# Edge lists loaded and keyed in two halves of columns, from two DMA queues, in a graph and mixture-of-experts kernel

## What is computed

```
def gnn(X, w_est, rows, cols):
    W = zeros((256, 256)).at[rows, cols].set(w_est)
    return X @ W

def ffn(x, gamma, beta, Wr, br, W1, b1, W2, b2):
    xn = layernorm(x) * gamma + beta
    logits = xn @ Wr + br                       # 8 experts
    top_vals, top_idx = top_k(logits, 2)
    w_full = softmax(top_vals) spread over the 8 experts
    y = 0
    for e in range(8):
        h = gelu(xn @ W1[e] + b1[e])            # 256 -> 512
        y = y + (h @ W2[e] + b2[e]) * w_full[:, e]
    return y

x = x + gnn(layernorm(x), edge_weight, src, dst)
x = x + ffn(layernorm(x), gamma, beta, Wr, br, W1, b1, W2, b2)
```

## Time and profile before

| | us |
|---|---|
| timed runs | 1067.57, 1066.40, 1067.41 (median 1067.41) |
| profiled execution, its own time | 1067.55 |
| its span, first to last instruction | 1065.8 |
| busy: TensorE / VectorE / ScalarE / GpSimd | 902.6 / 753.5 / 633.5 / 630.5 |
| mean granted TensorE clock, share of full speed | 0.919 |

### The profile page before, as it was taken

The page is one execution under the profiler, slowest core; times in us unless marked ns, Lnnn a source line. Parts: engine busy times, 40 slices in busy tenths (PEclk is TensorE's granted clock), DMA queues, the critical chain, the costliest instruction groups (busy, mean ns, idle before and its releaser), DMA issues. The chain is left out here.

```text
span 1065.8 us, 25585 instructions
## 1 busy us (share of the span) xinstructions
PE 902.6 (85%) x6756; PEld 842.6 (79%) x6757; DVE 753.5 (71%) x2311; ACT 633.5 (59%) x1324; POOL 630.5 (59%) x490
## 2 busy tenths in 40 slices
PE   1494698898986109999999999999999999999991
PEld 1123577777765109999999999999999999999991
DVE  4995798999984606777777777777777777777761
ACT  2244567666654006667667667667677677677661
POOL 3645057777777752465655655655756565656653
PEclk9797798989986559999999999999999999999996
DMA  4144457757654443465554554554654554555542
GB/s 123 56 127 150 135 161 228 225 195 243 210 168 158 148 162 72 73 99 87 82 95 73 93 94 80 82 96 73 93 92 79 83 95 79 92 85 81 93 67 30
DMA packets 95923, 121.47 MB, mean 114 GB/s; under 512 B 15198, under 2 KB 73734, under 8 KB 95752
## 3 DMA queue, kind: packets, MB, share of 16 engines
q0 software_dynamic: 39904, 53.56, 29.1%
q1 hardware_dynamic: 55976, 67.43, 21.9%
HBM read 51.94 MB, written 69.00 MB: 113 GB/s over the span
## 5 line engine op out<-in xcount | busy, mean ns | idle before, releaser
L574 POOL DMA_INDIRECT out_dram<-ysb,yid x210 | 382.6, 1822 | 283.6 <-ACT ysb L1342 132.9
L744 PE MATMUL psum<-xh,w1s 128*128 128x256 f32 x1680 | 310.9, 285 | 0.0
L744 PEld LDWEIGHTS psum<-xh,w1s 128*128 128x128 f32 x1680 | 257.1, 189 | 0.0
L558 POOL DMA_INDIRECT slots<-arena_z,pos x196 | 191.8, 978 | 89.8 <-issue 58.8
L757 PE MATMUL psum<-w2h,hl 128*128 x840 | 237.5, 283 | 0.0
L757 PE MATMUL psum<-w2l,hh 128*128 x840 | 237.3, 283 | 0.0
L757 PE MATMUL psum<-w2h,hh 128*128 x840 | 237.2, 282 | 0.0
L744 PE MATMUL psum<-xl,w1s 128*128 128x256 f32 x840 | 235.3, 280 | 0.0
L1159 DVE TENSOR_TENSOR hl<-hact,hh 128x512 fp32r<-128x512 f32 x210 | 145.6, 693 | 88.0 <-ACT hh L1206 87.8
L1206 ACT ACTIVATE xh<-psum 128x512 fp32r<-128x512 f32 x105 | 62.7, 597 | 221.3 <-PE psum L731 221.3
L1325 ACT ACTIVATE hact<-psum,b1T 128x256 f32<-128x256 f32 x420 | 174.5, 466 | 14.2 <-PE psum L744 2.8
(11 more groups left out here) (186 smaller groups left out, 1123.8 us busy)
## 6 DMA issues: line engine op xcount, KB each, us to landing
zin<-slots SPq DMA_DIRECT2D x105, 260.0 KB
arena_x<-in_x_dram SPq DMA_DIRECT2D x14, 512.0 KB, 5.4
out_dram<-arena_s SPq DMA_DIRECT2D x14, 512.0 KB
arena_z<-in_L_ffn_W_dram SPq DMA_DIRECT2D x24, 256.0 KB, 2.8
arena_x<-in_x_dram SPq DMA_DIRECT2D x13, 384.0 KB
out_dram<-arena_s SPq DMA_DIRECT2D x13, 384.0 KB
out_dram<-ysb,yid POOLq DMA_INDIRECT x210, 4.3
slots<-arena_z,pos POOLq DMA_INDIRECT x196
```

Of the source, the lines that this page charges most:

```text
L558: pool.indirect_dma_start(slots[:, :], bass.IndirectOffsetOnAxis(ap=pos[b][0:n, k, s:s + 1], axis=0), zg[b][0:n, s, :], None).then_inc(sen ...
L574: pool.indirect_dma_start(out[:, :], bass.IndirectOffsetOnAxis(ap=yid[u % MB][:, n:n + 1], axis=0), ysb[u % YB][:, n, :], None, compute_op ...
L744: last = nc.tensor.matmul(bank[2 + 2 * b + q][:, m * PAIR:(m + 1) * PAIR], w1s[b][:, w, k, hb * P:(hb + 1) * P], xs[b][:, k * PAIR:(k + 1) ...
```

## The change

The loads of src go out on SyncE's queue, those of dst on ScalarE's. Each list is loaded in two halves of columns (0 to 895 and 896 to 1699, seven blocks of 128 each, the last one short), each half still in two DMAs by rows. Each half has its own semaphore `raw_in[h]`, and VectorE makes the keys of the first half before it waits for the second. `keys_ready` is raised once for each half, and TensorE waits for it at block 0 and at block 7. The router constants stand ahead of the waits for `block_out` and `scratch_ready` instead of behind them. ScalarE runs a copy of one column into `first_gelu` before the first copy from PSUM, and the table load comes with that. What is computed stays the same.

```
--- before.py
+++ after.py
@@ -23,6 +23,7 @@
 EBLK = -(-ECOLS // P)
 ELAST = ECOLS - (EBLK - 1) * P
 EPARTS = ((0, 112), (112, EROWS))
+EHALF = ((0, 7 * P), (7 * P, ECOLS))
 HALF = 2
 EARLY = 1
 ROW0 = 9
@@ -267,7 +268,7 @@
         s_const = sem("s_const")
         dve_passed = sem("dve_passed")
         pool_passed = sem("pool_passed")
-        raw_in = sem("raw_in")
+        raw_in = [sem(f"raw_in{h}") for h in range(2)]
         small_in = sem("small_in")
         keys_ready = sem("keys_ready")
         score_zeroed = sem("score_zeroed")
@@ -350,15 +351,18 @@
         x_tiled = x[0:(TILES - 1) * P, :].rearrange("(n p) d -> p n d", p=P)
         out_tiled = out[0:(TILES - 1) * P, :].rearrange("(n p) d -> p n d", p=P)
 
+        def load_edges(engine, a, i):
+            rows = a.rearrange("(p c) -> p c", p=EROWS)
+            for h, (left, right) in enumerate(EHALF):
+                for lo, hi in EPARTS:
+                    engine.dma_start(raw[i].bitcast(a.dtype)[lo:hi, left:right], rows[lo:hi, left:right]).then_inc(raw_in[h], 16)
+
         block = ctx.enter_context(nc.Block())
 
 
         @block.sync
         def _(sp):
-            for i, a in enumerate((src, dst)):
-                rows = a.rearrange("(p c) -> p c", p=EROWS)
-                for lo, hi in EPARTS:
-                    sp.dma_start(raw[i].bitcast(a.dtype)[lo:hi, :], rows[lo:hi, :]).then_inc(raw_in, 16)
+            load_edges(sp, src, 0)
             sp.dma_start(wr[:, :, :], Wr.rearrange("(k p) e -> p k e", p=P)).then_inc(small_in, 16)
             with nc.allow_non_contiguous_dma(reason="two values a partition"):
                 sp.dma_start(gam[:, :], gamma.rearrange("(k p) -> p k", p=P)).then_inc(small_in, 16)
@@ -597,8 +601,9 @@
 
 
             pe.wait_ge(s_const, 4)
-            pe.wait_ge(keys_ready, 1)
             for i in range(EBLK):
+                if i % 7 == 0:
+                    pe.wait_ge(keys_ready, i // 7 + 1)
                 m = P if i < EBLK - 1 else ELAST
                 nc.tensor.transpose(bank[i // 4][0:m, (i % 4) * P:(i % 4) * P + EROWS],
                                     key_raw[:, i * P:i * P + m], ident[0:EROWS, 0:EROWS]).then_inc(block_turned, 1)
@@ -784,27 +789,27 @@
         @block.vector
         def _(dve):
             v = nc.vector
-            dve.wait_ge(raw_in, 32 * len(EPARTS))
             t = Steps(dve, edge_step, 0)
-
-
-            outer = junk[0:EROWS, 0:ECOLS]
             src_i, dst_i = raw[0].bitcast(I32), raw[1].bitcast(I32)
-            t.did(v.tensor_tensor(outer, src_i, dst_i, ALU.max))
-            t.then(v.scalar_tensor_tensor(out=src_i, in0=src_i, scalar=8, in1=dst_i, op0=ALU.logical_shift_left, op1=ALU.bitwise_or))
-            dve.wait_ge(s_const, 1)
-            t.then(v.tensor_tensor(src_i, src_i, place_raw, ALU.bitwise_or))
-            v.scalar_tensor_tensor(out=key_raw, in0=outer, scalar=float(D), in1=key_raw, op0=ALU.is_lt, op1=ALU.mult).then_inc(keys_ready, 1)
-            dve.wait_ge(block_out, 4)
+            for h, (left, right) in enumerate(EHALF):
+                def half(a):
+                    return a[0:EROWS, left:right]
+                dve.wait_ge(raw_in[h], 32 * len(EPARTS))
+                t.did(v.tensor_tensor(half(junk), half(src_i), half(dst_i), ALU.max))
+                t.then(v.scalar_tensor_tensor(out=half(src_i), in0=half(src_i), scalar=8, in1=half(dst_i), op0=ALU.logical_shift_left, op1=ALU.bitwise_or))
+                if h == 0:
+                    dve.wait_ge(s_const, 1)
+                t.then(v.tensor_tensor(half(src_i), half(src_i), half(place_raw), ALU.bitwise_or))
+                v.scalar_tensor_tensor(out=half(key_raw), in0=half(junk), scalar=float(D), in1=half(key_raw), op0=ALU.is_lt, op1=ALU.mult).then_inc(keys_ready, 1)
             dve.wait_ge(s_const, 4)
-            dve.wait_ge(scratch_ready, 1)
-
             dve.wait_ge(small_in, 80)
             for k in range(KD):
                 v.tensor_scalar(wrg[:, k, :], wr[:, k, :], gam[:, k:k + 1], None, ALU.mult)
                 v.tensor_copy(bet_e[:, k, :, :].rearrange("p a b -> p (a b)")[:, 0:E * E:E + 1], bet[:, k:k + 1].to_broadcast([P, E]))
                 last = v.tensor_scalar(betb[:, k, :], ones[:, :], bet[:, k:k + 1], None, ALU.mult)
             last.then_inc(wrg_ready, 1)
+            dve.wait_ge(block_out, 4)
+            dve.wait_ge(scratch_ready, 1)
             v.tensor_scalar(junk, score, 0.0, None, ALU.is_gt, ALU.add, accum_out=n_edge[:, :]).then_inc(n_edge_ready, 1)
             dve.wait_ge(n_edge_turned, 1)
             t.then(v.tensor_reduce(n_maxf[:, :], bank[5][0:1, 0:P], AX.X, ALU.max))
@@ -1204,7 +1209,9 @@
         def _(act):
             def copy(out_, in_):
                 return nc.scalar.activation(out_, in_, ACT.Copy)
+            load_edges(act, dst, 1)
             act.wait_ge(s_const, 4)
+            copy(first_gelu[:, :], ident[:, 0:1])
 
             act.wait_ge(score_zeroed, 1)
             tv = score.rearrange("p (b r) -> p b r", b=EBLK)
```

3 lines of the change are left out of this document (2 added, 1 removed).

## The result

| | before | after |
|---|---|---|
| median of the runs, us | 1067.49 (1065.48 to 1068.36, 6 runs) | 1061.89 (1061.05 to 1063.72, 6 runs) |
| ratio of after to before | | 0.9954, 95% interval 0.9941 to 0.9967 |
| profiled span, us | 1065.8 | 1059.3 |
| first key pass starts, us | 9.73 | 6.85 |
| count starts, us | 22.72 | 17.58 |

What follows compares the result with a forecast made beforehand. TensorE was taken to bound the expert stage and GpSimd most of the group stage, both behind one start chain; 3.0 + 1.6 + 0.65 + 0.8 = 6.05 us off that chain gave 1061.4 us, range 1059.6 to 1064.8.

Steps and rivals of the forecast that it cites:

- What bounds the kernel, and that the start carries to the end: Whole kernel: TensorE paces the expert stage, GpSimd most of the group stage; a gain at the count reaches the end.
- Rival C: Behind the count: the gain is spent on one or two further slow picks, 1.8 us each; 1063.2 to 1065.0; chance 0.11.
- Rival D: At the picks: four of the other seven turn slow too, 7.2 us lost against 6.05 gained; 1068.6; chance 0.04.
- The loads: List loads at the start: first halves moved at 4.85 us, VectorE starts at 6.1 instead of 9.73.
- rival A: List loads: halves less far apart or VectorE held; first pass at 7.9 to 8.7 us, 1063.0 to 1064.0; chance 0.18.
- The passes: VectorE's keys: eight passes of 1.10 and 1.00 us take 8.3, keys end at 14.4 instead of 17.43, 3.0 us gained.
- the price of nothing: VectorE's first passes beside GpSimd's constants until 8.70 us: no cost taken, against a bound of 2.6 us.
- The turns: TensorE's block turns: seven of fourteen remain behind the keys, ending at 16.1 instead of 20.72 us; 1.6 us gained.
- The copies and the table load: ScalarE's copies behind the last turn: with the table loaded early, only the last short pair remains; 0.65 us gained.
- The router constants: VectorE ahead of the count: six instructions of 0.81 us now fill its wait; 0.8 us gained.
- The clearing: GpSimd's clearing (0.52 us) moves with the last turn, ends at 16.7 beside ScalarE's 16.6; costs up to 0.1 us.
- The sum: Start to count: 3.0 + 1.6 + 0.65 + 0.8 = 6.05 us gained, count at 16.7 us, time 1061.4 us.

Runs made afterwards that it cites:

- the one-queue kernel: The changed kernel with all list loads on SyncE's queue, first halves of src and dst before the second halves; 1061.88 us, ratio 0.9943 to the kernel before.
- the last kernel: The changed kernel in three parts, clearing early, with the picks' index row read from PSUM and the flag instruction removed; 1051.32 us, ratio 0.9826 to the kernel before.

## Why the prediction was right, point by point

**What bounds the kernel, and that the start carries to the end.** Right. The first scatter moved by 5.81 and the first expert turn by 5.79 us for 5.14 at the count, the median by 5.6; a delay of 6.2 us at the numbers cost 7.0. The groups' and experts' durations didn't change: the 196 scatters show 191.6 and 59.1 us against the earlier trace rows. The 0.6 to 0.7 us by which scatter and turn moved beyond the count's own 5.14 are within the spread of the stretch behind the numbers (109.1 to 113.1 us). Rival C's cause, a second or third pick with slow products, shows in no trace of the study; what spreads behind the numbers is something else, in part the held columns. Rival D is out: the first pick's products took 3.78 us and the other seven 1.98 or 1.99 in both kernels.

**The loads.** The step that was off in size. VectorE started at 6.85 instead of 6.1. The byte curve was right to 0.25 us (5.1 instead of 4.85). The other 0.5 us are a wrong reading of the curve: it counts every row, and I took its first 0.896 MB for the first halves, while their last row ended at 5.81. The tail itself was as before: 1.04 us from the last row's end, against 1.03. So rival A's picture, rows of src's second half ahead of rows of dst's first, was partly true, and small. Its cause, the mixing of two queues, isn't shown: one queue gave 7.00 and the same overlap. Its sign, a first pass after 7.5 us, came in one of six executions with these loads (7.76); the other five had 6.83 to 7.19.

The Trainium skill's rule of 9 to 17 descriptors (DMA: Bandwidth & Descriptors, "Queues, rings and completion order") would let an engine take all of its first-half rows of src before one of dst, if a row is one descriptor. The trace doesn't agree with that reading: by 3.5 us 62 of src's 125 first-half rows had begun and 38 of dst's. With the Trainium skill (DMA: Bandwidth & Descriptors, "Rules for kernel authors"), by which a second issuing engine gives no bandwidth, the traces agree: 0.87 MB had begun by 5.0 us in the changed kernel on two queues, 0.95 in the kernel before and 0.80 in the one-queue kernel.

**The passes.** Right: 1.09 and 0.99 us forecast as 1.10 and 1.00, eight in 8.22 us for 8.3. Beside GpSimd's writes they took what they took later alone, 1.09 at 6.85 and at 10.10, so the price of nothing stood. With that the trace agrees with the Trainium skill (SBUF — State Buffer, "Who interferes with whom"), by which two-input passes aren't held by instructions that only write.

**The turns.** Right: 16.85 for the last, 1.78 us behind the keys for 3.29 before, 1.5 us gained for 1.6.

**The copies and the table load.** The sum was right, the label wrong. 0.65 us were gained behind the last turn less the clearing's 0.2, but the experiment without the early load lost nothing: the pause between the halves hides it. This part of the change could be left out.

**The router constants.** Right, 0.81 us. **The clearing.** Too cheap: I gave up to 0.1 us, it is 0.19, since it starts when the last block is turned and ends at 17.43, ScalarE's last copy at 17.36; with the clearing early the count stood 0.19 us nearer to the first pass.

**The sum.** 2.88 (start) − 0.52 (longer passes) + 1.51 (turns) + 1.27 (copies and constants, less the clearing) = 5.14, where I had 3.63 − 0.6 + 1.6 + 1.45. That the forecast time was nearer than the forecast count is luck: the stretch behind the numbers happened to be 0.7 us shorter in the changed kernel's trace than in the other, within its spread.

## What to carry to other kernels

Where an engine idles for the whole of a load, cut the load and the work on it into the same parts and let each part have its semaphore; here the parts gave the gain and a second queue none. The byte curve alone puts a part's end too early, since rows of the next part go ahead: here by 0.7 us, and the whole way from the curve to VectorE's start was 1.6 to 2.3 us in the seven executions with halves. Before a stall is put to its neighbours on the chain, look at what the other engines run during it: taking a 128x8 instruction of 7 us off the chain, with the columns' holds, brought the finished table 5.9 us forward, more than the whole change brought the count, though only 3.3 us of it reached the expert stage.

## What the runs showed of the hardware that I had not expected

- VectorE's `tensor_scalar` with its input in SBUF can be held not for one GpSimd split but for several that follow each other: 6.92 us over 128x8 elements, 3.59 us over 128x7 in the last kernel, each time until GpSimd paused. A column instruction at 61.95 in the kernel before got through between two splits. With the input in PSUM none of the 24 column instructions was held: 0.53 or 0.54 us each, beside a split or not.
- The same loads on two queues instead of one, whole columns: the first pass started at 10.74 and 11.47 us instead of 9.73 and 9.94, two executions each.
- Parts of a load overlap even on one queue: there 62 of the 250 second-half rows began before the last first-half row had ended (5.04 to 6.17 us). From a part's last row to the start of the instruction that waits for it were 0.8 to 1.4 us in mid-traffic and 0.6 to 1.3 at the end of traffic.
- TensorE's granted clock reads 1.00 until 32 us in the kernel before, yet its fp32 products of L619 took 0.89 us at 25.80 and 0.51 at 59.77: in that early stretch the column didn't tell the speed; the clock's first record in that trace stands at 29.2 us.
- Leaving out the tile `alive`, 32 bytes in each partition, should have moved the tiles allocated behind it, and the down products' weight loads fell from 191 to 188 ns, the expert stage by 5.8 us. That the addresses are the cause is argued from what else was the same; no run moved them alone, so it stays open.
